# One-core ViT tower kernel: small per-step work placed later among the expert slots

## What is computed

```python
h = einsum('bnk,dk->bnd', patches(x), W) + b                 # embedding of 8x8 patches
# recurrence over the images; each token is a row of the batch
h_new = tanh(layernorm(h)[t] @ W_ih.T + b_ih + b_hh + h_prev @ W_hh.T)
h = h + h_new
# mixture of 16 experts, the best 2 weighted, on x2 = layernorm(h)
gate_logits = x2 @ gate_w + gate_b ; top 2, softmax -> weights
hid = relu(einsum('bsh,ehf->bsef', x2, w1) + b1) ; expert_out = einsum('bsef,efh->bseh', hid, w2) + b2
y = x2 + weighted sum of the best two
h = h + layernorm(y) * gamma + beta
```

## Time and profile before

| | |
|---|---|
| three timed runs | 583.43, 583.30, 582.72; median 583.3 us |
| the profiled execution | 584.91 us, its span 583.1 us |
| mean granted TensorE clock | 0.985 |
| busy share of the span | PE 92%, DVE 74%, ACT 61%, POOL 29% |
| chain that ended last | PE 78%, DVE 5%, ACT 5%, DMA 4% |

### The profile page before, as it was taken

The page is one execution under the profiler, slowest core; times in us unless marked ns, Lnnn a source line. Parts: engine busy times, 40 slices in busy tenths (PEclk is TensorE's granted clock), DMA queues, the critical chain, the costliest instruction groups (busy, mean ns, idle before and its releaser), DMA issues.

```text
span 583.1 us, 8948 instructions
## 1 busy us (share of the span) xinstructions
PE 534.7 (92%) x3138; PEld 358.0 (61%) x3138; DVE 430.0 (74%) x819; ACT 356.2 (61%) x596; POOL 170.2 (29%) x133
## 2 busy tenths in 40 slices
PE   2577999999999999999999999999999999999991
PEld 2365666576666767576666767576666657565640
DVE  1144868978787878978787888878787797886762
ACT  2236665767567674757667675757667475846561
POOL 4122011513132241513242241523232151311334
PEclk9999999999999999999999999999999899998996
DMA  3304683563819184562909174562809265462801
GB/s 79 95 15 107 146 191 75 137 145 74 194 31 233 32 181 101 125 156 63 203 22 229 46 177 105 121 161 65 203 18 219 60 142 125 107 146 71 184 0 42
DMA packets 30140, 67.45 MB, mean 116 GB/s; under 512 B 7056, under 2 KB 12432, under 8 KB 29968
## 3 DMA queue, kind: packets, MB, share of 16 engines
q1 hardware_dynamic: 30096, 66.89, 49.4%
HBM read 59.59 MB, written 7.28 MB: 115 GB/s over the span
## 4 chain that ended last, share of the span: by engine, by line
PE 78%; DVE 5%; ACT 5%; DMA 4%; issue 4%; POOL 2%; SPq 1%; POOLq 0%; DVEq 0%; ACTq 0%
PE pZ L711 29%; PE pO L724 28%; PE pA L660 4%; PE pA L735 4%; PE pB L635 4%; DMA xcur<-x_in 4%; ACT hexp L426 2%; PE pA L653 2%; PE pB L686 2%; PE pA L645 2%; PE pA L675 1%; DVE acc L559 1%; POOL inv_std L327 1%; SPq L293 1%; PE pB L695 1%
## 5 line engine op out<-in xcount | busy, mean ns | idle before, releaser
L426 ACT ACTIVATE hexp<-pZ,b1c 128x784 f32<-128x784 f32 x256 | 229.5, 908 | 83.1 <-PE pZ L711 80.9
L543 DVE SCALAR_TENSOR_TENSOR prod<-pO,b2c,spread 128x392 f32<-128x392 f32 x256 | 151.6, 623 | 98.4 <-PE pO L724 91.8
L724 PE MATMUL pO<-hexp,w2s 128*64 128x392 f32 x1024 | 199.8, 506 | 1.3 <-ACT hexp L426 1.3
L711 PE MATMUL pZ<-xt,w1hi 128*128 128x392 f32 x512 | 194.8, 380 | 3.7 <-ACT hexp L426 2.3
L711 PE MATMUL pZ<-xt,w1lo 128*128 128x392 f32 x512 | 175.7, 343 | 0.0
L711 PEld LDWEIGHTS pZ<-xt,w1hi 128*128 128x128 f32 x512 | 97.5, 190 | 64.1 <-issue 36.2
L327 POOL TENSOR_TENSOR inv_std<-var,nhalf 112x7 f32<-112x7 f32 x48 | 74.7, 1566 | 174.5 <-DVE var L477 174.5
L724 PEld LDWEIGHTS pO<-hexp,w2s 128*64 128x64 f32 x1024 | 70.4, 137 | 79.2 <-issue 63.9
L559 DVE TENSOR_TENSOR acc<-acc,prod 128x784 f32<-128x784 f32 x112 | 118.4, 1057 | 0.1
L711 PEld LDWEIGHTS pZ<-xt,w1lo 128*128 128x128 f32 x512 | 97.9, 191 | 0.0
L334 POOL TENSOR_TENSOR h2b<-h2c,bet 112x448 f32<-112x448 f32 x16 | 20.2, 1263 | 169.0 <-DMA h2c<-h_dram 169.0
(11 more groups left out here) (74 smaller groups left out, 425.6 us busy)
## 6 DMA issues: line engine op xcount, KB each, us to landing
spread<-gates_dram SPq DMA_DIRECT2D x128, 392.0 KB, 9.0
h_dram<-h SPq DMA_DIRECT2D x16, 199.1 KB, 2.5
h2c<-h_dram SPq DMA_DIRECT2D x16, 199.1 KB, 9.7
xcur<-x_in SPq DMA_DIRECT2D x16, 196.0 KB, 9.9
out<-yo SPq DMA_DIRECT2D x16, 196.0 KB, 9.3
w1f<-w SPq DMA_DIRECT2D x2, 512.0 KB, 6.1
w2s<-w SPq DMA_DIRECT2D x1, 512.0 KB, 6.8
gates_dram<-gt SPq DMA_DIRECT2D x16, 28.0 KB, 2.0
```

The source lines that it names most:

```text
L426: nc.scalar.activation(hexp[u % RING][:, :].rearrange("p (b c) -> p b c", b=2), halves(pZ[u % 2]), ACT.Relu, bias=b1c[:, u:u + 1])\
L543: nc.vector.scalar_tensor_tensor(out=prod[q % RING][:, b * HALF:(b + 1) * HALF], in0=halves(pO)[:, b, :], scalar=b2c[:, q:q + 1], in1=spre ...
L711: last = nc.tensor.matmul(halves(pZ[e % 2])[:, b, :], w[:, e, :], xt[par][:, b * HALF:(b + 1) * HALF], start=(k == 0), stop=(k == 1))
L724: last = nc.tensor.matmul(halves(pO)[k * D:(k + 1) * D, b, :], w2s[:, e, :], hexp[e % RING][:, b * HALF:(b + 1) * HALF], start=True, stop= ...
```

## The change

Only slot numbers and the place of a call change; no operation is added or removed.

| work | slot before | slot after |
|---|---|---|
| `embed_turn`, `keep_xn1t` | 2 | 3, on PE ahead of `logits` |
| `recur`, `new_hidden` | 3 | 5 (4 in the fill) |
| `hidden_turn` | 5 (4 in the fill) | 7 (5 in the fill) |
| `h2` on DVE | 5 | 7 |
| `embed_in`, `keep_h1` | 5 (3 in body -2) | 7 (4 in the fill) |
| `sum_turn` | 7 | 9 |
| squares on ACT: mix, close, embed | 7, 8, 9 | 9, 10, 11 |
| variances on DVE: mix, close, embed | 9, 10, 11 | 11, 12, 13 |
| `x2` on DVE, high part on ACT, low part on DVE | 12, 12, 14 | 13, 14, 15 |
| `close_norm` on ACT | 14 | 15 |

```diff
 # ACT
-                    if embed and u == (3 if known(t, -1) else 5):
+                    if embed and u == after(t, 4, 7):
                         keep_h1(t + 3, 1 - par)
-                    if mix and u == 2:
+                    if mix and u == 3:
                         keep_xn1t(t + 2)
-                    if mix and u == 3:
+                    if mix and u == after(t, 4, 5):
                         new_hidden(t + 2)
...
-                    if close and u == 14:
+                    if close and u == 15:
                         close_norm(t - 1)
-                    if mix and u == 12:
+                    if mix and u == 14:
                         MIX.wait(act, t + 2, "x2")
 # DVE
-                    if mix and u == 5:
+                    if mix and u == 7:
                         MIX.wait(dve, s, "hid_turned")
...
-                    if mix and u == 12:
+                    if mix and u == 13:
                         norm_scale(MIX, s, 1, x2[:, :, :], h2[:, :, 0:D])
 # PE
+                    if mix and u == 3:
+                        embed_turn(t + 2)
                     if gate and u == 3:
                         logits(t + 1, 1 - par)
-                    if mix and u == 3:
+                    if mix and u == after(t, 4, 5):
                         recur(t + 2)
...
-                    if mix and u == after(t, 4, 5):
+                    if mix and u == after(t, 5, 7):
                         hidden_turn(t + 2)
-                    if embed and u == (3 if known(t, -1) else 5):
+                    if embed and u == after(t, 4, 7):
                         embed_in(t + 3)
-                    if close and u == 7:
+                    if close and u == 9:
                         sum_turn(t - 1, 1 - par, mix)
...
-                    if mix and u == 2:
-                        embed_turn(t + 2)
```

More of the change, by code:

```diff
@@ L447, in body @@
                         nc.scalar.activation(gt[:, :], pB[0:2 * E, 0:FIRST], ACT.Copy).then_inc(GATE.sem, 1)
-                    if mix and u == 7:
+                    if mix and u == 9:
                         square(MIX, t + 2, "h2", 1, h2[:, :, 0:D])
-                    if close and u == 8:
+                    if close and u == 10:
                         close_center(t - 1)
                         square(CLOSE, t - 1, "center", 2, cen[:, :, :])
-                    if embed and u == 9:
+                    if embed and u == 11:
                         square(EMBED, t + 3, "kept", 0, h1[1 - par][:, :, 0:D])
-                    if close and u == 14:
+                    if close and u == 15:
                         close_norm(t - 1)
-                    if mix and u == 12:
+                    if mix and u == 14:
                         MIX.wait(act, t + 2, "x2")
@@ L587, in body @@
                         gate_weights(g)
-                    if mix and u == 9:
+                    if mix and u == 11:
                         norm_var(MIX, s, 1)
-                    if close and u == 10:
+                    if close and u == 12:
                         norm_var(CLOSE, c, 2)
-                    if embed and u == 11:
+                    if embed and u == 13:
                         norm_var(EMBED, a, 0)
-                    if mix and u == 12:
+                    if mix and u == 13:
                         norm_scale(MIX, s, 1, x2[:, :, :], h2[:, :, 0:D])
-                    if mix and u == 14:
+                    if mix and u == 15:
                         MIX.wait(dve, s, "hi")
```

## The result

| | before | after |
|---|---|---|
| runs side by side, median (lowest to highest) | 583.37 us (582.72 to 584.47, 4 runs) | 574.06 us (573.36 to 577.03, 4 runs) |
| ratio, 95% interval | | 0.985 (0.981 to 0.989) |
| profiled execution, span | 584.91, 583.1 | 573.36, 571.6 |
| first layer 1 to the next, steady | 32.86 | 32.04 |
| turn of x2 of step 0 | 51.28 | 53.40 |

The account below looks back on a forecast made before the run. PE's own work was taken to bound the kernel, with about 1.2 us of stalls per 32.86 us period. Terms summed to -10.9 on the profiled run (574.0), -8.8 from the median (574.5); forecast 574.2, range 570 to 580.5.

Parts of the forecast that it names:

- start, to x2's turn: Ahead of step 0: gates 1.2 us later, x2 held 0.5 more; plus 1.7, bounds minus 0.6 to plus 3.
- step 0, from there: Step 0: two stalls go (0.59, 0.35), a new one comes (0.27); minus 0.7 us.
- steps 1 to 12, embedding's gap and clock with them: Shorter steady periods give minus 10.9 us; the embedding's gap and lower clock, minus 2.1, in the profiled run only.
- step 13: Step 13: no embedding covers the second search, about 0.75 lost against 0.9 won elsewhere; minus 0.2 us.
- step 14: Step 14: `sum_turn` now behind the 1.50 stall, plus 1.4; the `close_norm` stall goes, minus 0.6; together plus 0.8 us.
- end: Last work: `h2c` fetch starts 0.8 later, POOL's last `rstd` stands behind `add_beta`; plus 0.5 us (0 to 0.8).
- The steady step: Three PE stalls become one of 0.27 us, bound by the chain of x2; period 31.94 instead of 32.86.
- The embedding: Embedding two slots later: its load gets 0.5 to 2 us more air, so the gap there goes (0.4).
- the sentence on VectorE's fast modes: At the start: if the first small operation of `gate_weights` ran in a fast mode, 0.6 us more.
- rival 2: POOL's `add_beta` blocks DVE's second search; 1.5 us more would cost 0.8 in 12 steps, 584; chance 0.03.
- rival 1: Thin covers (`hexp` 11, turn of xn, second product) fail by 0.3 to 0.7 a step: 578 to 582; chance 0.2.
- rival 3: Chain of x2 longer than laid out, each 0.1 us lengthening every step by 0.1; up to 593; chance 0.07.

Follow-up runs that it names:

- Few moves: Kernel before, steady steps only: turn of xn slot 3, recurrence 4, x2's high part 14, low part 15, `close_norm` 15; embedding stays. 582.26 us, ratio 0.997.
- The start in the order of before: Changed kernel with the two bodies ahead of step 0 in the order of the kernel before: 573.43 us, ratio 0.984.
- before with the early load: Kernel before, with SP issuing the patches' load ahead of the gates' spread in the step before instead of behind the store: 581.97 us, ratio 0.997.
- turn of xn with recurrence: Kernel before, steady steps only: turn of xn and its copy moved to slot 3, recurrence and tanh to 4: 582.31 us, ratio 0.997.
- split early: Changed kernel with ACT's high part of the w1 split moved ahead of the copy of x's turn, before step 0: 573.22 us, ratio 0.984.

## Why the prediction was right

By the terms of its sum, from first layer 1 to the next, in the two profiles:

| term | predicted | measured |
|---|---|---|
| start, to x2's turn | +1.7 | +2.1 (51.28 to 53.40) |
| step 0, from there | -0.7 | -0.6 (28.90 to 28.26) |
| steps 1 to 12, embedding's gap and clock with them | -10.9 - 2.1 = -13.0 | -12.2 (396.73 to 384.55) |
| step 13 | -0.2 | -0.2 (31.58 to 31.34) |
| step 14 | +0.8 | -1.6 (31.73 to 30.11) |
| end | +0.5 | +1.0 (42.90 to 43.91) |
| sum | -10.9 | -11.5 (583.1 to 571.6) |

The sum is nearer than its terms. They were off by +0.4, +0.1, +0.8, 0, -2.4 and +0.5, and these cancel to -0.6. So the nearness of the number is in part luck: at step 14 a fall of the clock in the profiled run of before (1.7) makes up for three terms that were too hopeful.

**The steady step was right, and by its mechanism.** Two stalls are gone, one is left, and it is bound by the chain of x2. The period is 32.04 for 31.94: `x` and `hexp` 15 are 0.1 later than laid out. That the chain bounds is shown by experiment and not only by the rows: x2 ahead of the variance won 0.36 a step, `close_norm` in 14 lost 1.0.

**The embedding was right in direction, and its weight was not seen.** The load got its air (patches now land 2.3 to 3.0 us ahead of need, 0.04 to 0.8 before). The prediction gave it 0.5 to 2 us more, on the ground that load and embedding both move. The load is issued 1.9 later in the step (4.47 behind first layer 1, 2.61 before, in the middle of steps 2 to 12), but it lands where it did (12.63 behind it, 12.59 before), so nearly the whole 2.6 by which the embedding moved is air. The page after has:

```profile
xcur<-x_in SPq DMA_DIRECT2D x16, 196.0 KB, 8.1
```

The prediction counted the air as one gap of 0.4 and one fall of the clock. Few moves shows it to be a condition for the rest: without it, the steps that got shorter by 0.8 ran into the landing of the load, and with the clock's falls all was lost. The same kind of sum, made for few moves, gave 572.5 to 576, and 582.26 came.

**The start was mis-sized by 0.4.** `gates_turn` came at 48.91, where 48.4 stood, because already L520 was held; the sentence on VectorE's fast modes gave 0.6 for it. By that rule of the Trainium skill (SBUF — State Buffer, section "SBUF: two separate sides") an operation in such a mode that comes second waits for the whole GpSimd instruction, and the trace agrees in the time: 3.03 beside POOL's L354, 0.16 without. In which mode L520 ran no trace says. The start in the order of before takes the whole 2.1 back, but it moves the embedding, the split and the square together; no run has the embedding's place alone.

**Step 14 failed, with the wrong sign.** There are two errors. The clock had fallen a second time in the kernel before, at 525.2, and the prediction overlooked it although its row is 0.69 long where 0.44 is normal. It cost 1.7, and the changed kernel has no such fall there. It need not be the change's doing: before with the early load kept the same wait of 1.50 and had no fall. And PE's wait was 2.03, not 2.9, because the search ran 0.45 into POOL's beta instead of 1.3. The 1.4 for `sum_turn` itself was sized from the place it left: back in slot 7 it gave step 14 only 0.55 of it, since then the search was held again.

**The end was mis-sized by 0.5**, by a cause that was not in it: the last turn of the sums took 2.88 instead of 1.59 at the lower clock. Up to there it was 0.3 better than before. The prediction's own reason failed too: POOL's last `rstd` waited for the variance and not for beta, which had ended at 562.81.

```profile
563.23 1.49 POOL L327 TENSOR_TENSOR inv_std<-var,nhalf 112x7 f32<-112x7 f32 x1 [0.42 <-DVE var L477]
```

**Rivals.** The second search does meet POOL in nine of the steps 1 to 12 (not in 5, 8 and 10), as rival 2 said: DVE and POOL of the changed kernel,

```profile
255.13 1.15 DVE L498 TENSOR_TENSOR hit<-lg,tv 112x112 f32<-112x112 f32 x1
256.32 0.99 DVE L500 TENSOR_TENSOR hit<-hit,rank 112x112 f32<-112x112 f32 x1
```

```profile
255.08 1.07 POOL L334 TENSOR_TENSOR h2b<-h2c,bet 112x448 f32<-112x448 f32 x1 [9.13 <-DMA h2c<-h_dram]
256.23 0.95 POOL L337 TENSOR_TENSOR h2b<-h2b,h2c 112x448 f32<-112x448 f32 x1
```

and `hexp` 7 ended 0.4 us ahead of need, so it costs nothing there. It decides only where no embedding covers it, in steps 13 and 14. None of the thin covers failed (rival 1), and of rival 3 only 0.1 a step came. Rival 2's own 584 lies within the 1.2 us of 583.3 that the prediction calls no change, so its chance belonged to "same" and not to "slower".

What stays open: what decides whether a given wait lets the clock fall, and whether the medians would keep the start's 2.1 us, which 4 or so runs each don't settle.

## What to carry to other kernels

A load that lands just in time is no stall, and no row shows it as one, yet it is the next bound: before you shorten a loop by 0.8 us, take the margin of every transfer in it and subtract the 0.8. When several small stalls make up a loss, look for what each of them hides; here one of them alone was worth 0.2 us a step, and all but one were worth nothing, and an edit of the order on the DMA queue was worth 13 us behind the others and 1.8 without them. When an operation is moved away from a POOL instruction that blocks it, say what stands in that instruction's way next, at the start, the end and in the last steps apart.

## What was not expected of the hardware

- TensorE's clock fell from 2.4 to 1.2 GHz, for 3.4 us, at the same places of some runs and not of others. Ahead of an embedding (14 matmuls of 65 columns) it fell behind idle times of 0.26, 0.34, 0.48 and 0.55 us and not behind 0.25, 0.29, 0.30, 0.32, 0.33, 0.46, 0.63 and 0.94 (before, few moves, and turn of xn with recurrence). Ahead of expert 9 in step 14 it fell behind 1.50 (before), 2.46 (start in the order of before) and 2.47 (close_norm in 14), and not behind 1.50 (before with the early load), 2.03 (changed) or 2.77 (split early). The length of the wait alone does not decide it.
- The same load of 196 KB took 7.5 to 9.9 us to land (medians of twelve profiles) when issued behind the spread of the gates, and 3.3 and 3.4 us ahead of it. Behind it, issuing 1.9 us later did not move the landing.
- VectorE's operation on 7 elements a lane was held for 3 us by one GpSimd instruction, while a reduction (L496, 0.26 us, at 41.35 in the start of before's order) and h2's addition out of PSUM (0.63) beside the same instruction were not.
- The clock's rise at the start is not tied to the work alone. In seven profiles step 0's first matmul starts at 47.8 to 47.9, and the clock rose at 50.2 to 56.3; with a start at 49.5 to 49.6 (three profiles) it rose at 51.9, 52.7 and 58.4, with 46.7 (one) at 54.4, and with 44.7 to 44.8 (three) at 48.2, 48.2 and 49.0.
